# Attention with the maxima of the next turn: in steps that hold only maxima, both move behind the second score pair

## The reference, cut to what matters

```python
B, N, C = x.shape                                   # 2, 1024, 288
h = _modulate(_ln(x), sh_msa, sc_msa)
qkv = (h @ w_qkv + b_qkv).reshape(B, N, 3, nh, hd).transpose(2, 0, 3, 1, 4)
q, k, v = (qkv[0], qkv[1], qkv[2])
attn = jax.nn.softmax(jnp.einsum('bhqd,bhkd->bhqk', q, k) * hd ** (-0.5), axis=-1)
o = jnp.einsum('bhqk,bhkd->bhqd', attn, v).transpose(0, 2, 1, 3).reshape(B, N, C)
...
gate_logits = xf @ w_gate
topk_logits, topk_idx = jax.lax.top_k(gate_logits, TOP_K)
hmid = jax.nn.gelu(jnp.einsum('tc,ech->eth', xf, w1) + b1[:, None, :], approximate=True)
eo = jnp.einsum('eth,ehc->etc', hmid, w2) + b2[:, None, :]
return x + g_mlp[:, None, :] * moe
```

## Time and profile before

| | |
|---|---|
| median of 3 runs | 948.18 us (947.07 to 959.93) |
| the profiled execution | 946.91 us, span of its instructions 945.1 us |
| granted TensorE clock, mean | 0.939 |
| TensorE busy | 827.9 us (88%) |
| VectorE busy | 568.5 us (60%) |
| ScalarE busy | 476.4 us (50%) |
| GpSimd busy | 341.3 us (36%) |
| attention, first score to last V | 110.9 to 522.4 us |

### The profile page before, as it was taken

How to read it: one execution, slowest core, us unless ns; L and a number is a source line. 1 busy time by engine, 2 the same in 40 slices (tenths; PEclk the granted TensorE clock), 3 DMA queues, 4 the chain that set the end, 5 groups by cost and what they waited for, 6 DMA issues and landing times. The chain is left out here.

```text
span 945.1 us, 15242 instructions
## 1 busy us (share of the span) xinstructions
PE 827.9 (88%) x5111; PEld 554.2 (59%) x5111; DVE 568.5 (60%) x994; ACT 476.4 (50%) x975; POOL 341.3 (36%) x348
## 2 busy tenths in 40 slices
PE   4886799999999999999988885369999999999995
PEld 3683333333333333333322563259999999999995
DVE  3765878777787778778860493825455434434432
ACT  0540267666676676667777364344334333333331
POOL 6534221131212222110422298066555444344332
PEclk9896799999999999999999795579999999999998
DMA  8021120424131221203222394134332222222221
GB/s 219 10 57 28 40 49 20 88 83 92 22 85 23 63 51 34 65 8 84 78 55 66 110 285 153 53 109 113 81 64 36 39 46 37 38 45 38 38 37 20
DMA packets 56384, 62.98 MB, mean 67 GB/s; under 512 B 24184, under 2 KB 50662, under 8 KB 55736
## 3 DMA queue, kind: packets, MB, share of 16 engines
q1 hardware_dynamic: 47304, 49.30, 20.1%
q0 software_dynamic: 8400, 12.12, 7.7%
q10 hardware_dynamic: 608, 0.59, 0.2%
HBM read 33.87 MB, written 15.73 MB: 52 GB/s over the span
## 5 line engine op out<-in xcount | busy, mean ns | idle before, releaser
L1064 DVE TENSOR_REDUCE negmax<-m_ps 128x2 f32<-128x1024 f32 x256 | 306.5, 1221 | 73.9 <-PE m_ps L1132 73.7
L1033 ACT ACTIVATE probs<-s_ps 128x512 f32<-128x512 f32 x512 | 269.8, 602 | 105.3 <-PE s_ps L1165 105.2
L1165 PE MATMUL s_ps<-stack 56*128 56x512 f32 x512 | 161.5, 476 | 21.2 <-ACT probs L1033 21.2
L1165 PEld LDWEIGHTS s_ps<-stack 56*128 56x128 f32 x512 | 65.5, 185 | 181.8 <-ACT probs L1033 154.6
L1132 PE MATMUL m_ps<-stack 54*128 54x512 f32 x512 | 136.6, 452 | 15.2 <-DVE negmax L1064 7.9
L1179 PE MATMUL o_ps<-probs,v_aug 128*19 128x512 f32 x1024 | 136.4, 605 | 6.3 <-ACT o_sb L1040 5.1
L2013 PE MATMUL gate_bank<-weights,ht_hi 128*128 x630 | 127.1, 296 | 0.4 <-DVE ht_lo L1909 0.4
L1989 PE MATMUL h_ps<-weights,xt_hi 128*128 x525 | 115.3, 350 | 4.6 <-DVE xt_hi L1902 4.6
L995 POOL CAST parts<-proj_f 128x512 fp32r<-128x512 f32 x28 | 17.1, 610 | 261.9 <-ACT proj_f L1025 129.3
L1687 POOL DMA_INDIRECT out<-res,ido x35 | 56.9, 1624 | 140.5 <-DVE res L1931 140.5
L1735 ACT CAST ht_hi<-ht_ps 128x384 fp32r<-128x384 f32 x105 | 43.6, 488 | 119.7 <-PE ht_ps L2000 119.7
(11 more groups left out here) (213 smaller groups left out, 1117.9 us busy)
## 6 DMA issues: line engine op xcount, KB each, us to landing
stack<-parts SPq DMA_DIRECT2D x96, 144.0 KB
w_raw<-in_L_cond_w SPq DMA_DIRECT2D x9, 432.0 KB
w_raw<-in_L_cond_w SPq DMA_DIRECT2D x9, 384.0 KB
xn_scratch<-h SPq DMA_DIRECT2D x16, 192.0 KB, 3.7
x_in<-in_x SPq DMA_DIRECT2D x4, 576.0 KB, 8.6
o_scratch<-o_norm SPq DMA_DIRECT2D x16, 144.0 KB, 2.4
o_in<-o_scratch SPq DMA_DIRECT2D x16, 144.0 KB, 2.6
xr<-in_x SPq DMA_DIRECT2D x16, 144.0 KB, 3.0
```

What stands on the lines that cost most here:

```text
L1033: nc.scalar.activation(probs[:, st % 2, h], s_ps[k % S_BANKS][:], ACT.Exp, scale=SCALE)\
L1064: nc.vector.tensor_reduce(negmax[:, half, first:first + count], m_ps[n % 2][:], AX.X, ALU.max, negate=True)\
L1165: nc.tensor.matmul(s_ps[k % S_BANKS][:], stack[s][r, j, 1, kt // QT, (kt % QT) * P:(kt % QT + 1) * P], stack[s][r, j, 0, half], start=True ...
```

## The change

The plan, the banks and the other engines' orders stay. Only TensorE's order within a step is changed, and only in steps without a projection all of whose items are maxima ("plain" steps below, the others "mixed"): both items go behind the second scores, and none stands between the first scores and V.

```diff
                     items = plan.steps[STEPS * g + st]
+                    unit = PROJ_AT.index(st) if st in PROJ_AT and g + 2 < GG else None
+                    plain = unit is None and all(kind == "max" for _, kind, *_ in items)
                     scores(g, st, 0)
-                    for it in items[:1]:
-                        item(*it)
+                    if not plain:
+                        for it in items[:1]:
+                            item(*it)
                     if st >= 1:
                         values(g, st - 1)
                     elif g >= 1:
                         values(g - 1, STEPS - 1)
                     scores(g, st, 1)
-                    for it in items[1:2]:
+                    for it in items[0 if plain else 1:2]:
                         item(*it)
-                    unit = PROJ_AT.index(st) if st in PROJ_AT and g + 2 < GG else None
```

## The result

The changed kernel takes 970.03 us (median of 4 runs, 969.16 to 970.63), before 947.63 (4 runs, one more than in the table of before): ratio 1.0204, 95% interval 1.0121 to 1.0287. It is slower by 22 us, where I forecast 952, no change. The profiled execution took 969.16 us, its span 967.3 (before 945.1).

The account below looks back on a forecast made before the run. The attention step was taken as bound by a ring of latencies between TensorE, exponentials and reductions. Gains 17.7 and costs 21.8 made net +4.1 us on the profiled 946.91; with 1.3 for the median, forecast 952, range 943 to 960.

Parts of the forecast that it names:

- Plain behind plain: Plain step following a plain one: V to V 2.65 us for 2.83, gain 0.18 us at 31 places.
- a mixed step behind a plain one: Its first maxima pair waits for a reduction: V to V 3.47 us for 2.83, cost 0.64 at 29 places.
- the plain steps that the copy sets: Plain steps where V waits for ScalarE's copy of the output bank, 3.22 us: no gain, 9 places.
- the mixed ones that it sets: Mixed steps behind plain ones where the copy already sets 3.22 us: cost 0.25 us at 5 places.
- the transpose in group 7: Rowmax transpose in step 4 waits for both reductions of step 3: V at 4.65 against 3.55, cost 1.1 us.
- Behind a projection: Plain step after a projection step loses a maxima pair ahead of V: gain 0.33 us at 19 places.
- Behind the rowmax step: Plain step after a rowmax transpose without projection: V at about 2.78 for 2.83, gain 0.05 us, 8 places.
- the start: Group 0's step 0 at half clock: moving its first maxima pair costs 0.8 us, between 0 and 1.3.
- The lone score matmuls: Slow rival: score matmuls without maxima beside them cost their slot, plain-after-plain steps stay near 2.83; 958 to 959, chance 0.06.
- The range's other slow rival: A plain step's first reduction starts 0.23 later, so each of 29 waits costs 0.87 us: 959, chance 0.16.
- the clock rival: TensorE idler at each wait, clock falls to 1.2 GHz, costing 7 us and more: 968 and above, chance 0.03.

Follow-up runs that it names:

- experiment 7: Changed kernel with every maxima reduction over half of its keys (256 of each 512, work left out): 932.32 us, ratio 0.9827.
- experiment 2: Kernel before, with the new order in group 7's plain steps (0, 1 and 3) alone: 966.05 us, ratio 1.0192.
- experiment 4: Kernel before, with the new order in step 3 of group 7 alone: 964.58 us, ratio 1.0177.
- experiment 5: Changed kernel with the rowmax transpose of group 7's step 4 moved behind the second scores: 952.32 us, ratio 1.0055.
- experiment 6: Changed kernel with seven unread score matmuls added ahead of the rowmax transpose in group 7's step 4: 957.93 us, ratio 1.0087.
- experiment 9: Kernel of experiment 6 with two unread maxima matmuls more in each of group 7's steps 6 to 15: 951.74 us, ratio 1.0031.
- experiment 8: Changed kernel, new order in groups 0 to 5 only, not step 11; projection steps' maxima also moved later: 936.58 us, ratio 0.9876.
- experiment 10: Kernel of experiment 8 with two unread maxima matmuls more in each of group 7's steps 6 to 15: 934.08 us, ratio 0.9852.
- experiment 3: Changed kernel with step 3 of group 7 in its order of before: 962.01 us (951.51 to 963.02), ratio 1.0121.

## Why the prediction was wrong

- **The steps: right.** Plain behind plain was 2.65 to 2.66 us (forecast 2.65), a mixed step behind a plain one 3.47 (3.47), the plain steps that the copy sets 3.23 (no gain forecast), the mixed ones that it sets 3.46 to 3.48 (3.47), the transpose in group 7 4.68 (4.65). The wait for a reduction is shown as the cause by experiment 7.
- **Small sizes off.** Behind a projection the gain was 0.22 to 0.24, not 0.33: V follows the score pair there by 0.43 (407.85 to 408.28), where I had 0.33. It isn't the kind of pair: behind the output step, where a maxima pair runs ahead of the scores, V follows them by 0.33 (489.92 to 490.25). Over 19 places that is 2 us. Behind the rowmax step V to V was 2.72, not 2.78. Group 0 came out 1.6 us longer with its start, where my terms make 1.3; but single executions can't price the start, since in experiment 2, whose group 0 is as before, group 1 began as late as in the changed kernel (169.15; changed 169.14, before 167.54), the clock having risen at 119.2 in place of 115.7. Up to group 7 the sum was 4.4 us, forecast 3.0 (4.1 without group 7's 1.1). With group 7's 1.1, which came out as forecast, the steps' own cost is 5.5 us for 4.1.
- **The lone score matmuls** cost nothing: plain steps behind plain ones took 2.65 us. ScalarE's exponential of S3 ends at 433.79 and V starts at 433.84, so V waits for it in any case. By the Trainium skill (TensorE: Matmul & The Clock Gate, Part 3, "The mechanism") small matmuls on different rows of the array run side by side. The trace of before agrees with it (both at 311.31 in the earlier trace rows), but the cost that I weighed from it doesn't appear. The range's other slow rival, a reduction that starts later, is out too: the wait was over when forecast.
- **The step that failed** is the clock rival, put at 0.03, with its argument "in the last 31 us of attention it was busy for 24.67 only, and the granted clock stayed at 1.00". A mean over 31 us, without a standstill among it, said nothing of 1.8 us in one piece, which the same text had just worked out (a transpose at 4.45 behind scores at 2.17), and put at 1.1 us only. Experiments 2 and 4 show that with this wait the kernel takes 18.0 and 16.5 us more than before, in all eight executions; 5 and 6 that it is TensorE's idleness in it, and not the lateness; 9 that with the later gaps filled as well 4 us remain. The price was off too: I had 14 us of work at half clock for 7 us and more, and it was 61 us (496.4 to 557.8) where before had 13.6.
- **What the table of before already held**: one execution of three at 959.93, which the prediction passes over. With nothing added to group 7's steps without maxima such executions, some 12 us longer at a clock of 0.92, are nine of 52 of the kernel before and four of ten in experiment 8; experiments 9 and 10, with these steps filled, have none in 16. What one looks like can be seen in experiment 3, whose profiled execution is 10 us longer than its shortest: half clock from 511.7 on. That the long executions of before are the same event is likely by their clock, but there is no trace of one.

Left open: why the clock holds in one execution of the same kernel and falls in the next, and what decides the place.

## What to carry to other kernels

Where TensorE's order is changed, look for the longest standstill that it makes, and for what comes after it. Here 1.1 us more of wait, ahead of a stretch in which TensorE was busy for 24.67 of 31 us, cost 16.5 us. A spread in the times of the kernel before, with a lower mean clock in the long runs, is a reason to ask where the clock falls in them. Unread matmuls in the waits that are there anyway are a way to test it, and here a remedy as well. And with two banks between two engines, a pair that is moved late makes the next early one pay, so move that as well.

## What the runs showed of the hardware

One wait of 1.83 us on TensorE, with only two matmuls moved, was followed within 2 us by a granted clock of 0.50 in place of 1.00, for the 47 us left of attention (experiment 4), though TensorE was then busy for 42.31 of 46 us: being busy again didn't bring it back there. In experiment 2 the clock fell inside the same wait, 0.7 us before its end. In experiment 6 it did come back after 20 us, in steps of the same kind. In experiment 9 matmuls that nobody reads, in the rowmax wait and in the waits of 0.45 us of the steps without maxima, went with 1.00 to the end of attention in the traced execution and a mean clock of 0.940 or more in all twelve, and cost no time in those steps: V to V stayed at 2.65 to 2.67 us.
